# Layer 0's pairs in six chunks of up to 128 rows and one of 40, whose high and low parts are stacked for one f32r pass

## What is computed

```
X0 = stack of 39 looked-up rows          # (512, 39, 16)
Xi = X0
for W, b in ((W0,b0), (W1,b1), (W2,b2)): # W: (128, 39*Fi)
    Xi = einsum('hjk,bjd,bkd->bhd', W.reshape(128, 39, Fi), X0, Xi) + b[None, :, None]
    res.append(Xi.sum(axis=2))
h = relu(concat(res + [dense]) @ W_top1 + b_top1); h = relu(h @ W_top2 + b_top2); y = h @ W_top3
```

## Time and profile before

| | us |
|---|---|
| median of 3 runs | 684.92 (683.94 to 685.0) |
| the profiled execution | 690.58 |
| its span, first to last instruction | 688.7 |
| mean granted clock of TensorE | 0.993 |

### The profile page before, as it was taken

The page is one execution under the profiler, slowest core; times in us unless marked ns, Lnnn a source line. Parts: engine busy times, 40 slices in busy tenths (PEclk is TensorE's granted clock), DMA queues, the critical chain, the costliest instruction groups (busy, mean ns, idle before and its releaser), DMA issues.

```text
span 688.7 us, 10364 instructions
## 1 busy us (share of the span) xinstructions
PE 660.6 (96%) x2686; PEld 485.6 (71%) x2686; DVE 511.2 (74%) x977; ACT 566.0 (82%) x1997; POOL 443.9 (64%) x437
## 2 busy tenths in 40 slices
PE   4499999999999999999999999999999999999998
PEld 4376767577777777777777777777777777777683
DVE  5387887677777877777877777787777787888780
ACT  3387877789888988888898889888888888999672
POOL 6558375687877778777778878777787736433000
PEclk9799999999999999999999999999999999999999
DMA  6222143322334343332321313131313122003400
GB/s 209 65 62 50 6 100 67 78 68 56 105 89 97 97 95 96 68 97 22 110 39 30 73 10 92 7 96 8 97 6 98 5 89 84 2 1 133 165 1 0
DMA packets 107532, 46.02 MB, mean 67 GB/s; under 512 B 80897, under 2 KB 92941, under 8 KB 107474
## 3 DMA queue, kind: packets, MB, share of 16 engines
q1 hardware_dynamic: 101427, 42.82, 23.5%
q0 software_dynamic: 5120, 1.29, 2.1%
q10 hardware_dynamic: 927, 1.26, 0.7%
HBM read 13.81 MB, written 5.24 MB: 28 GB/s over the span
## 4 chain that ended last, share of the span: by engine, by line
PE 87%; ACT 3%; issue 2%; POOL 2%; DMA 2%; DVE 2%; SPq 1%; another core or an unknown queue 0%; ACTq 0%; DVEq 0%; POOLq 0%
PE ps_y L956 20%; PE ps_y L958 19%; PE ps_y L957 19%; PE ps_x L884 13%; PE ps_g L973 4%; ACT prod L599 2%; PE ps_tr L853 2%; PE ps_y L1019 1%; PE ps_y L1018 1%; PE ps_y L1017 1%; PE ps_y L1031 1%; DMA room<-room 1%; POOL room L419 1%; PE ps_y L967 1%; PE ps_y L898 1%
## 5 line engine op out<-in xcount | busy, mean ns | idle before, releaser
L599 ACT ACTIVATE prod<-ps_y,xt 128x128 f32<-128x128 f32 x1792 | 492.5, 442 | 78.4 <-PE ps_y L958 72.0
L956 PE MATMUL ps_y<-w_hi,x_hi 128*128 128x512 f32 (+1 forms) x640 | 311.6, 487 | 5.9 <-DVE prod L780 3.0
L957 PE MATMUL ps_y<-w_lo,x_hi 128*128 128x512 f32 (+1 forms) x640 | 249.0, 389 | 0.0
L958 PE MATMUL ps_y<-w_hi,x_lo 128*128 128x512 f32 (+1 forms) x640 | 248.9, 389 | 0.0
L424 POOL TENSOR_TENSOR prod<-prod 128x512 f32<-128x512 f32 x112 | 144.4, 1289 | 110.8 <-ACT prod L599 104.5
L780 DVE SCALAR_TENSOR_TENSOR prod<-ps_y,xt,prod 128x128 f32<-128x128 f32 x576 | 164.0, 344 | 48.7 <-PE ps_y L958 47.0
L395 POOL DMA_INDIRECT rows<-in_table,index x160 | 155.2, 970 | 58.7 <-issue 27.5
L787 DVE TENSOR_REDUCE prod<-prod 128x128 f32<-128x1536 f32 (+1 forms) x64 | 120.6, 1884 | 63.8 <-ACT prod L599 63.6
L956 PEld LDWEIGHTS ps_y<-w_hi,x_hi 128*128 128x128 f32 x640 | 120.5, 188 | 64.6 <-issue 21.5
L957 PEld LDWEIGHTS ps_y<-w_lo,x_hi 128*128 128x128 f32 x640 | 120.7, 189 | 46.4 <-issue 23.4
L419 POOL TENSOR_TENSOR room<-room 117x512 f32<-117x512 f32 (+1 forms) x105 | 134.9, 1290 | 11.1 <-DMA room<-room 11.0
(11 more groups left out here) (118 smaller groups left out, 318.5 us busy)
## 6 DMA issues: line engine op xcount, KB each, us to landing
room<-room SPq DMA_DIRECT2D x75, 234.0 KB
room<-room SPq DMA_DIRECT2D x45, 78.0 KB
emb_room<-rows SPq DMA_DIRECT2D x168, 5.0 KB
rows<-in_table,index POOLq DMA_INDIRECT x160
w_hi_dram<-g_all SPq DMA_DIRECT2D x5, 512.0 KB
w_lo_dram<-g_all SPq DMA_DIRECT2D x5, 512.0 KB
room<-room SPq DMA_DIRECT2D x15, 156.0 KB
g_all<-in_L_rec_W SPq DMA_DIRECT2D x9, 256.0 KB, 6.4
```

Of the source, the lines that this page charges most:

```text
L599: ins = nc.scalar.activation(prod[:, SLOT[k] + m // 2, :, m % 2], ps_y[:, g % YBANKS, m * H:(m + 1) * H], ACT.Copy, scale=xt[:, q % 2, ti, ...
L956: nc.tensor.matmul(y, hi, w1_hi[:, cols], start=True, stop=False)
L957: nc.tensor.matmul(y, hi, w1_lo[:, cols], start=False, stop=False)
L958: nc.tensor.matmul(y, lo, w1_hi[:, cols], start=False, stop=True).then_inc(y_made, 1)
```

## The change

The pairs are dealt differently. The three shifts of a chunk are now 6 apart (`STEP`), which gives six chunks of 117 rows with shifts 0 to 17; eleven more rows (`EXTRA`) of the shares fill chunks 0 to 3 up to 128, 127, 126 and 125 rows. What is left are 40 pairs in four runs of ten (`RUNS`), chunk `LAST`. Their left factors go to a tile of their own (`left`, room in `g_hi`) and their right factors to `bz[:, LAST]`, by two transfers a run.

From quad 4 on (`STACKED_FROM`) chunk LAST is summed otherwise: ScalarE rounds the product to f32r (`z_stack`, rows 0 to 39), VectorE takes the rest (`z_low`), and two transfers stack high, high and low part on 120 partitions. Against weights stacked as high, low and high (`w0_stack`, made once), one f32r pass sums all three terms.

So per quad the passes of layer 0 stay seven, of which one is f32r from quad 4 on; SyncE's queue gets a fourth share and eight runs, one window less and two stacking copies. In the first tile one selection pass more stands on TensorE and more small copies stand in VectorE's prologue. The positions of the layer-0 passes and the order of the products change with it. The core of the diff:

```diff
-CHUNKS = -(-SHIFTS // SPC)
-XROWS = REP + CHUNKS - 1
+XROWS = P
+STEP = 6
+CHUNKS = STEP + 1
+LAST = STEP
+EXTRA, EXTRA_CHUNKS = 21, 4
+RUN = 10
+RUNS = [(32, 50), (11, 29), (31, 50), (11, 30)]
+LEFT_ROWS = RUN * len(RUNS)
...
-SUMMED_AFTER = {(0, 2): 0, (0, 5): 1, (0, 8): 2, (1, 1): 3, (1, 8): 4, (2, 8): 5, (3, 2): 6}
+SUMMED_AFTER = {(0, 2): 0, (0, 8): 1, (1, 1): 2, (1, 8): 3, (2, 2): 4, (2, 8): 5, (3, 2): LAST}
...
 def chunk_rows(c):
-    return F * sum(c + CHUNKS * a < SHIFTS for a in range(SPC))
+    return LEFT_ROWS if c == LAST else P - c if c < EXTRA_CHUNKS else REP
+def share_parts():
+    return [(F * a, F * (a + 1), -STEP * a % F) for a in range(SPC)] + [(REP, P, EXTRA)]
...
             def share_rows(q, landed):
                 wait(sp, z_made, CHUNKS * q)
+                for a, b, at in share_parts():
+                    sp.dma_start(xa[a:b, :], x0[at:at + b - a, q % 2, :]).then_inc(landed, 16)
+            def load_runs(q, landed):
...
+                for n, (l, r) in enumerate(RUNS):
+                    at = slice(RUN * n, RUN * (n + 1))
+                    sp.dma_start(left[at, :], x0[l:l + RUN, q % 2, :]).then_inc(landed, 16)
+                    sp.dma_start(bz[at, LAST, :], x0[r:r + RUN, q % 2, :]).then_inc(landed, 16)
+            def stack(q):
+                sp.wait_ge(z_lo_made, q - STACKED_FROM + 1)
+                sp.dma_start(z_stack[LEFT_ROWS:2 * LEFT_ROWS, :].bitcast(F32),
+                             z_stack[0:LEFT_ROWS, :].bitcast(F32)).then_inc(z_stacked, 16)
+                sp.dma_start(z_stack[2 * LEFT_ROWS:, :].bitcast(F32), z_low.bitcast(F32)).then_inc(z_stacked, 16)
...
                 share_rows(q, shared[q % 2])
-                for c in range(1, CHUNKS):
+                if q >= STACKED_FROM:
+                    load_runs(q, runs_ld[q % 2])
+                for c in range(1, LAST):
                     cut_window(q, c, cut[q % 2])
+                if q < STACKED_FROM:
+                    load_runs(q, runs_ld[q % 2])
                 if q + 1 < QUADS:
                     lay_out(q + 1)
...
+                if q >= STACKED_FROM:
+                    stack(q)
...
             def multiply(q, c):
...
                 if c == 1:
-                    wait(pool, cut[q % 2], 16 * (CHUNKS - 1) * ((q + 1) // 2))
+                    wait(pool, cut[q % 2], 16 * (LAST - 1) * ((q + 1) // 2))
+                if c == LAST:
+                    wait(pool, runs_ld[q % 2], 16 * 2 * len(RUNS) * ((q + 1) // 2))
...
+            def split_last(q):
+                act.wait_ge(z_made, CHUNKS * q + multiplied(q).index(LAST) + 1)
+                if q > STACKED_FROM:
+                    act.wait_ge(z_used, CHUNKS * q)
+                nc.scalar.copy(z_stack[0:LEFT_ROWS, :], bz[0:LEFT_ROWS, LAST, :]).then_inc(z_hi_made, 1)
...
+                if ti == SPLIT_LAST_AFTER[0] and STACKED_FROM <= q + 1 < QUADS:
+                    n = q + 1 - STACKED_FROM
+                    dve.wait_ge(z_hi_made, n + 1)
+                    wait(dve, z_stacked, 32 * n)
+                    nc.vector.tensor_tensor(z_low, bz[0:LEFT_ROWS, LAST, :], z_stack[0:LEFT_ROWS, :].bitcast(F32),
+                                            ALU.subtract).then_inc(z_lo_made, 1)
...
+                if c == LAST and q >= STACKED_FROM:
+                    pe.wait_ge(w0_stacked, 32)
+                    pe.wait_ge(z_stacked, 32 * (q - STACKED_FROM + 1))
+                    w, z = w0_stack[:], z_stack
...
-            for c in range(1, CHUNKS):
-                ins = nc.tensor.matmul(ps_y[0:REP, (c - 1) // 2, (c - 1) % 2 * P:((c - 1) % 2 + 1) * P],
-                                       ident[0:XROWS, c:c + REP], first, start=True, stop=True)
+            for c in range(1, LAST):
+                ins = nc.tensor.matmul(ps_y[:, (c - 1) // 2, (c - 1) % 2 * P:((c - 1) % 2 + 1) * P],
+                                       window[:, c:c + P], first, start=True, stop=True)
...
+            for side in range(2):
+                ins = nc.tensor.matmul(ps_y[0:LEFT_ROWS, 3, P * side:P * (side + 1)],
+                                       pick_runs[:, LEFT_ROWS * side:LEFT_ROWS * (side + 1)], first, start=True, stop=True)
```

More of the change, by code:

```diff
@@ L108 @@
 RING = 4
-SYM = F + CHUNKS - 1
+SYM = F + STEP - 1
 def wait(engine, semaphore, value):
@@ L182, in build @@
         g_lo = [x[:, par, :] for par in range(2) for x in (x1_hi, x1_lo)]
+        left = g_hi[0:LEFT_ROWS, 1, :].bitcast(F32)
+        z_low = g_hi[0:LEFT_ROWS, 2, :]
+        z_stack = g_hi[0:3 * LEFT_ROWS, 0, :]
+        w0_stack = sb("w0_stack", [3 * LEFT_ROWS, H], F32R)
+        w0_low = sb("w0_low", [LEFT_ROWS, H], F32R)
         xt = sb("xt", [P, 2, QT, F])
@@ L199, in build @@
         y_row = flat_prod[:, 0:B]
-        w0_sym = flat_prod[:, 0:CHUNKS * REP]
+        w0_sym = flat_prod[:, 0:CHUNKS * P]
         wt1 = emb_room[:].rearrange("p (c m) -> p c m", m=M1)
@@ L265, in build, with share_rest @@
         block = ctx.enter_context(nc.Block())
-        def share_rest(queue, a):
-            at = -CHUNKS * a % F
-            queue.dma_start(xa[F * a:F * (a + 1), P:], x0[at:at + F, 0, P:]).then_inc(first_shared, 16)
+        def share_rest(queue, part):
+            a, b, at = part
+            queue.dma_start(xa[a:b, P:], x0[at:at + b - a, 0, P:]).then_inc(first_shared, 16)
         def cut_rest(queue, c):
@@ L298, in share_rows @@
                 wait(sp, z_made, CHUNKS * q)
-                for a in range(SPC):
-                    at = -CHUNKS * a % F
-                    sp.dma_start(xa[F * a:F * (a + 1), :], x0[at:at + F, q % 2, :]).then_inc(landed, 16)
+                for a, b, at in share_parts():
+                    sp.dma_start(xa[a:b, :], x0[at:at + b - a, q % 2, :]).then_inc(landed, 16)
+            def load_runs(q, landed):
+                if q - 1 >= STACKED_FROM:
+                    sp.wait_ge(z_lo_made, q - STACKED_FROM)
+                else:
+                    sp.wait_ge(z_used, CHUNKS * (q - 1) + summed(q - 1).index(LAST) + 1)
+                for n, (l, r) in enumerate(RUNS):
[7 more added lines that the diff above has]
+                sp.dma_start(z_stack[2 * LEFT_ROWS:, :].bitcast(F32), z_low.bitcast(F32)).then_inc(z_stacked, 16)
             def cut_window(q, c, landed):
-                wait(sp, z_used, CHUNKS * (q - 1) + c + 1)
+                wait(sp, z_used, CHUNKS * (q - 1) + summed(q - 1).index(c) + 1)
                 n = chunk_rows(c)
@@ L317, in _ @@
             sp.wait_ge(x0_made, 1)
-            for a in range(SPC):
-                share_rest(sp, a)
-            for c in range(1, CHUNKS, 2):
+            for part in share_parts():
+                share_rest(sp, part)
+            for c in range(1, LAST, 2):
                 cut_rest(sp, c)
+            for n, (l, r) in enumerate(RUNS):
+                at = slice(RUN * n, RUN * (n + 1))
+                sp.dma_start(left[at, P:], x0[l:l + RUN, 0, P:]).then_inc(first_runs, 16)
+                sp.dma_start(bz[at, LAST, P:], x0[r:r + RUN, 0, P:]).then_inc(first_runs, 16)
             def load_w2(n):
@@ L494, in between @@
                 if q + 1 < QUADS:
-                    for c in MULTIPLIED_IN.get((ti, part), ()):
+                    for c in (MULTIPLIED_IN if q + 1 >= STACKED_FROM else FOURTH_MULTIPLIED_IN).get((ti, part), ()):
                         multiply(q + 1, c)
@@ L573, in _ @@
             act.wait_ge(first_xa_moved, 1)
-            nc.scalar.copy(xa[0:REP, 0:P], ps_g[0:REP, 0:P]).then_inc(first_xa, 1)
+            nc.scalar.copy(xa[:, 0:P], ps_g[:, 0:P]).then_inc(first_xa, 1)
             nc.scalar.copy(rest, turned[:, :, 1:, :]).then_inc(x0_made, 1)
             act.wait_ge(x0_made, 1)
-            for c in range(2, CHUNKS, 2):
+            for c in range(2, LAST, 2):
                 cut_rest(act, c)
@@ L615, in _ @@
                     scale(T, g)
+                    if (q, ti, g) == (1, 0, 4):
+                        nc.scalar.copy(w0_stack[0:LEFT_ROWS, :], w0t[0:LEFT_ROWS, LAST, :]).then_inc(w0_hi_made, 1)
+                    if STACKED_FROM <= q + 1 < QUADS and (ti, g) == SPLIT_LAST_AFTER:
+                        split_last(q + 1)
                     if g == 6 and ti == 1 and q + 1 < QUADS:
@@ L665, in _ @@
             ins.then_inc(ones_made, 1)
-            for a in range(SPC):
-                at = -CHUNKS * a % F
-                ins = nc.vector.tensor_copy(pick[:, F * a:F * (a + 1)], ident[:, at:at + F])
-            ins.then_inc(pick_made, 1)
+            for a, b, at in share_parts():
+                nc.vector.tensor_copy(pick[:, a:b], ident[:, at:at + b - a])
+            for n, (l, r) in enumerate(RUNS):
+                for side, at in enumerate((l, r)):
+                    nc.vector.tensor_copy(pick_runs[:, LEFT_ROWS * side + RUN * n:LEFT_ROWS * side + RUN * (n + 1)],
+                                          ident[:, at:at + RUN])
+            nc.vector.tensor_copy(window[:, 0:P], ident[:])
```

(1 more changed line is left out.)

117 lines of the change are left out of this document (76 added, 41 removed).

## The result

The changed kernel takes 893.86 us (median of 4, 892.85 to 894.13) against 684.96 us (683.94 to 692.17): 1.3031 times, 95% interval 1.2991 to 1.3071. The profiled execution has a span of 891.0 us and a mean granted clock of 0.885, where before had 688.7 and 0.993. It is 30% slower; 886 was forecast.

A forecast was written before the change was run, and what follows sets the result against it. TensorE, busy 96% of the span, was taken as the bound. Steady quads 158, quads 1 to 3 37.5 and the first tile 5.5 sum to +201 us: 886 from the median of 684.9, range 840 to 930.

The forecast's parts named there:

- The ring: Window transfers use the largest divisor of their rows up to 16 as rings; 127 rows get one, taking 16.1 us.
- The lone ring: Sign in the trace: the share of the rings is near one tenth for 10 us after each window.
- A steady quad: Quads 4 to 15: TensorE waits 11.7 us for GpSimd's chunk 1 product; a quad takes 48.1 us against 37.05.
- The clock: Behind each TensorE wait, 4.7 us at half speed cost 2.4 us; bounds 0 and 4.8.
- Rival (a): One ring, but the clock stays up or returns within a microsecond: 850 us, 843 with cheaper rows; chance 0.18.
- Quads 1 to 3 and the first tile: Late windows cost three times 10.1 us and 2.4 of clock, 37.5; the first tile's window 5.5 us.
- From the sum to the median: The sum of +201 puts the profiled execution's 690.6 us at 891.6; from the median of 684.9 it gives 886.
- Rival (c): Windows are spread over 13 or more rings after all: 685 us, no change; chance 0.09.
- The debt of 2.9 us in quad 2: Within the spread-windows case: quad 3's moves end 6 us later behind quad 2's runs, so transposes wait 2.9 us.
- What is taken from TensorE: One f32r pass replaces an f32 layer-0 pass in twelve quads from quad 4: 12 x 0.64 = 7.7 us.
- the rows of a chunk don't enter: Layer-0 passes on TensorE: 117 and 78 rows cost the same before, so 128 will too.
- Rival (d): Faster: twelve f32r passes at 0.64 us with windows in time, 680 us, 677 without the debt; chance 0.07.

The follow-up runs named there:

- e4: The changed kernel with 45 unread f32r passes ahead of the layer-0 pass at (0,8) of quads 3 to 14: 869.97 us, ratio 1.2581 to the kernel before.
- e1_rings: The changed kernel with two windows moved in two pieces, 127 rows as 126 + 1 and 125 as 120 + 5: 723.42 us, 1.0454 of the kernel before.
- e2: The changed kernel with only the 127-row window in two pieces, 126 + 1: 751.52 us, 1.0857 of the kernel before.
- e6: e1_rings with windows issued ahead of the eight runs in all quads and GpSimd's products reordered to match: 693.04 us, 1.0019 of the kernel before.
- e12: e6 unchanged, run again on another chip: 684.76 us, 0.9983 of the kernel before.
- e8: e6 with quad 2's runs issued behind the moves for quad 3, its 40-row product and pass later: 679.78 us, 0.9914 of the kernel before.
- e10: The kernel before with 128 columns in place of 123 in the transposes (XROWS), no other edit: 681.55 us, 0.9928 of the kernel before.
- e11: e8 with the pass over the stacked rows reading its operands as f32: 687.02 us, 1.0007 of the kernel before.
- e7: e6 with the stacked pass read as f32: 696.53 us, 1.0053 of the kernel before.
- e5: e1_rings with the stacked pass read as f32: 720.56 us, 1.0404 of the kernel before.

## Why the prediction held, and where it didn't

**The ring.** The largest divisor was concluded from 13 and 16, and it holds for the other counts that were run; the closing packets of a quad's windows are the 1 + 14 + 5 + 13 + 13 of the forecast, as the differences above show for the first three. The lone ring was to show for 10 us; it shows for 5 to 6, since the wider windows run beside it up to 516. The busiest ring was to be done at +27.0 with 179 rows at 0.09 us; the product started at +27.2. From 516.5 to 521.5, where the ring works alone, the trace has 62 rows of 2 KB, 12 a microsecond, and each takes 0.084. The forecast's product on chunk 1 and pass at +28.5 came at +27.2 and +28.5 (522.18 and 523.50 less 494.99).

**A steady quad.** 48.1 and 2.4 of clock make 50.5; it took 50.57. The rest of the quad, from the waiting pass to the next share, was 19.65 + 2.4 = 22.05 by the sum and is 545.56 - 523.50 = 22.06. The wait was to be 11.7 and is 11.8 in the row shown, 12.4 at the longest. That everything would stand behind GpSimd's product and nothing run ahead was right: VectorE's busy time in the wait is 0.00. The twelve quads together came 159.6 us longer than before, against 158 in the sum, and the four of them that turn W2 took 12.8 more on average, the other eight 13.5. Part of this match is chance: the transposes' gain of 0.4 to 0.6 us a quad (below) was missing from the sum. e4 shows the two parts of the 22.06. There the pass stood at +28.50 after the first share as well, and to the next share it took 19.44 us with the clock at 1.00:

```profile
512.46:531.90 19.44, 19.44 (x81) 14.44 (x82) 15.13 (x29) 15.29 (x56) 16.86 (x17) 1.00 0.11 13
```

So the work behind the pass was 0.2 us shorter than the 19.65 of the sum, and in this quad the low clock cost 2.6 and not 2.4: two small errors that cancel. Why the work is not shorter by the whole 0.4 to 0.6 isn't shown.

**The clock.** 2.4 us a wait was taken from the one stretch of before in which TensorE had stood. e4_fill gives the same mean, 13.3 less 10.9. Rival (a), that the clock stays up, fell with the first row of PEclk.

**Quads 1 to 3 and the first tile.** Three times 12.5 and 5.5 were 43.0; up to the end of quad 2 the kernel was 42.7 us behind (18.0 at the end of quad 0, 13.7 and 11.0 in the next two). VectorE's window of the first tile came 5.9 us late at TensorE, where 4.9 to 6.8 was the range:

```profile
40.35 1.65 PE L1067 MATMUL ps_x<-room,w0t 127*128 127x384 f32 x2 [5.90 <-DVE room L864]
```

**From the sum to the median** 1.9 us lay around the span and 5.7 us between the profiled execution of before and the median shown. The sum was +201, and the two spans differ by 202.3. But the 5.7 us were a matter of that one execution: the changed kernel's profiled execution took 892.85, 1.0 below its median. That is why 886 was 8 us low.

**Rival (c)**, the windows spread over 13 or more rings, was priced at 685, no change. e1_rings spreads them so, with two transfers more, and took 4.5% more than before. The step that didn't come is "the pass starts at +17.2 where it would arrive at +16.8". The two extra pieces put 1.6 us of issue in front; by (c)'s own sum that puts the product at +17.3 and the pass at +18.8. In e1 the product started 17.5 us after the first share (490.18 and 472.67 below), the pass came at +18.8, and it waited 1.5 us in this quad, up to 2.7 in others, in place of 0.4. So e1 doesn't refute the terms of (c), and no run has the windows on 13 rings or more without extra transfers; what e1 and e2 missed lies in their own expectations, which had the windows 1.0 and 1.4 us sooner than the products started and no low clock behind the wait. (In passing, (c) counts 627 rows where the five windows have 612, which is worth 0.1 us.) In e2 the product started at +18.7; the wait was 2.7 us in the quad shown, and behind it the clock fell. The mean granted clock was 0.981 in e1 and 0.964 in e2. So 1.2 us more of delay a quad cost another 4 points of the ratio, nearly 2 us a quad: the price of a late window isn't linear.

```profile
472.67 3.13 SPq L353 DMA_DIRECT2D room<-room  x4
...
481.93 5.45 SPq L376 DMA_DIRECT2D room<-room  x7
...
490.18 1.27 POOL L506 TENSOR_TENSOR room<-room 127x512 f32<-127x512 f32 x1 [2.01 <-DMA room<-room]
```

The stretch of e2_only127 behind such a wait, with its granted clock of 0.66:

```profile
552.35 1.96 PE L1018 MATMUL ps_x<-room,w0t 127*128 127x512 f32 x2 [2.70 <-POOL room L506]
...
551.00:556.00 5.00, 3.65 (x7) 2.23 (x8) 2.11 (x3) 0.49 (x3) 4.74 (x5) 0.66 0.24 8
```

The debt of 2.9 us in quad 2, named in (c), was there (2.8 and 2.9 us in e6 and e12), but it cost about 5 us (e12 against e8), since the clock fell behind it too; and e8 itself still waits 2.30 us in its place.

**What is taken from TensorE.** 0.64 us a quad for the f32r pass was right: 36.49 to 35.90 in one quad, and 7.2 (by the ratios 6.4) us in all against 7.7. The sentence "the rows of a chunk don't enter" was right as well (a 128-row and a 117-row product and pass take the same). Missed was that the change turns the transposes' 123 columns into 128: e10 puts 0.7% on that edit alone; the f32r pass gives 0.9% (e8 against e11). It stood in a constant of the diff (`XROWS`) and in the rows of before as `128*123`, with 0.94 us for four of them. The Trainium skill (TensorE: Matmul & The Clock Gate, section "Weight-path perf modes — Fast Weight Load (FWL) and DoubleRow") lets weights load fast only where there are 128 of them and the type is not FP32. The traces agree on the 128 (321 against 207 ns), but both loads here are f32, for which the page has no such gain. Whether that mode is at work here no run shows.

**Rival (d)**, faster with windows in time, was put at 680 with the debt and 677 without, 0.993 and 0.988 of before. e12 is at 0.9983 and e8 at 0.9914, where the forecast's 677, less the transposes' 4.9 us that it didn't have, would be 0.982 for e8. The first quads take most of the difference. e10 has the same transposes and ran on the same chip as e8; here are the first shares of quads 4 and 13 on SyncE's queue, in e8 and then in e10:

```profile
150.72 3.17 SPq L354 DMA_DIRECT2D room<-room  x4
...
476.99 3.13 SPq L354 DMA_DIRECT2D room<-room  x4
```

```profile
145.05 2.48 SPq L301 DMA_DIRECT2D room<-room  x3
...
476.93 2.48 SPq L301 DMA_DIRECT2D room<-room  x3
```

At quad 4 e8 is 5.7 us behind, and nine quads later it is level: 0.62 us a quad, the forecast's price of the f32r pass. Of the 5.7 us, 1.9 stand already at the first share of quad 1 (44.17 and 42.30), and 2.2 come between the first shares of quads 3 and 4, where the wait of 2.30 us for the 40 rows lies; the other 1.6 aren't traced to a wait. So (d) had the steady quad right, and what it lacked is the price of the first quads.

**Still open.** Why e6 had the 0.45 us wait for x_lo on one chip and, unchanged, not on another isn't shown. It could explain why e7 lost only 3.5 us, if the f32 pass filled a wait there; that is argued and not shown. And e5 against e1 shows no gain of the f32r pass at all: it lies ahead of the pass that waits for the windows.

## What to carry to other kernels

Count the rows of a transfer before anything else: the largest divisor up to 16 is the number of rings it gets, and a prime number of rows above 16 sends all of them down one (127 rows x 0.084 = 10.7 us here; shown for 113 and 127 rows). One row moved apart undoes it, at the price of one more issue. Where an operand grows by a few rows, look at who waits for its transfer, and put the transfers with an appointment ahead of those without one on the issuing queue. Price a wait of TensorE with the half clock behind it, and look at constants in a diff that change the shape of work which the change doesn't speak of.
